# Taps of a convolution read from PSUM, roots of three norms on GpSimd, a residual in another buffer

## The chip, the cores and the metric

The kernel runs on one core of one Trainium2 chip. The metric is the time of one execution on the device, in microseconds, the median of several runs. In the texts PE is TensorE, ACT is ScalarE, DVE is VectorE, POOL is GpSimd, and SP is the queue that issues the DMAs.

## The reference

4096 tokens (two sequences of 2048, 256 wide) pass four blocks, all in float32.

1. A selective state space block (Mamba). `xn = layer_norm(x)`, `xz = xn @ W_in`, split into `x_br` and `z` of 512 channels each. A causal depthwise convolution of 4 taps along time, `xb = silu(conv(x_br) + conv_b)`. From `xb` come `Bm`, `Cm` (16 states) and `delta = softplus(xb @ W_delta + b_delta)`. Then the recurrence `h = exp(delta * A) * h + delta * Bm * xb`, `y = sum(h * Cm)` over the 16 states, and `out = ((y + xb * Dp) * silu(z)) @ W_out + residual`.
2. A layer norm around a mixture of 4 experts with 2 chosen per token (router of one hidden layer, experts 256 to 1024 to 256, exact gelu).
3. An attention block of 16 heads of width 16, whose keys get an additional product term (`cross`).
4. A feed-forward block with its layer norms.

The convolution needs, for the first three tokens of a chunk, the last three of the chunk before, or zeros at the start of a sequence.

## The kernel before, in words

The program has two halves. The first, `mamba_moe_qkv`, does blocks 1 and 2 and the projections q, k, v of block 3, in 8 chunks of 512 tokens. The second half does attention and the feed-forward block; the change does not touch it.

The first half is a software pipeline whose order is written out by hand for each engine. In iteration `i` (from -1 to 9) the recurrence of chunk `i` runs in 16 slots `n`, one per state. In between stand the input side (norm, projection, convolution, delta) of chunk `f = i + 1`, the experts of chunk `m = i - 1` and q, k, v of chunk `q = i - 2`. Each engine goes through its instructions in order and waits on semaphores.

A slot of DVE is: `b_times` of half 0 (line 919, 128x1024, PSUM), two scans (line 930), whatever is placed in the middle of the slot, `b_times` and two scans of half 1, and `keep_state` (line 937); then what is placed at the end of the slot. POOL multiplies `h` by the row of C for that state (`times_c`, line 1132) and adds it to `y_sum` (`add_y`, line 1143); `h` has two buffers, so the scans of slot n need the sum of slot n-2. ACT makes the decays of slot n+1 (line 669) at the start of its slot n. PE makes the broadcast of a row of B (line 382) for slot n+2 at the end of slot n.

The parts that matter here, before the change:

- Layer norm (`layer_norm`, lines 53 to 87), wholly on DVE: four `bn_stats` (69), four `bn_aggr` (72), thirteen operations on 128x4 values for the inverse root (lines 75 to 82: a seed from the bits and three Newton steps), and four applies (84). norm0 is the input norm, of chunk `i + 2` at the end of slot 12; norm1 is of chunk `m` at the end of slot 2; norm2 of chunk `q` at the end of slot 1.
- The residual: `load_residual` (line 266) is issued by SP in slot 2, behind `load_c(i, 4)`, which waits for POOL's product of slot 2. It goes into `x1_tok`, the buffer in which norm1, the experts' sums and norm2 work. Line 948 adds it to the output projection (lines 435 to 446, `project_out`, PE in slot 1).
- Banks 4 and 5 of PSUM serve in turn `project_out`, the turning of x1 (`turn_x1`, 448), z (`project_z`, 405), the turning of xn (`turn_xn`, 385), the x projection (`project_x`, 394), the keys' addition (`add_keys`, 569, line 580), and the experts' `down` (502, line 518). The z projection and the silu gates stand in slot 3 on PE and ACT, `turn_xn` in slot 4, behind `turn_x1`; the x projection of blocks 0 and 1 in slot 4 behind `cross`, of blocks 2 and 3 in slot 5, ahead of `router` (456).
- The convolution: ACT copies each projected block from PSUM twice (`copy_x`, 692): as it is into `x_br`, three columns in (699), and scaled by the last tap's weight into `xb` (700). `halo` (860, DVE) puts the last three columns of the chunk before, or zeros, ahead of it. `conv` (868) adds the other three taps: twelve `scalar_tensor_tensor` per chunk (line 879), `xb += w * x_br[shifted]`, six at the end of slot 7 and six at the end of slot 9. ACT's silus (703) follow in slot 11. `x_br` is also the buffer `pre` of the delta projection (721).
- The experts' `up` (492) goes through banks 6 and 7 with ACT's gelu (740); `down` from slot 7 on; its results are read by DVE at line 1015 in the middle of slots 8 to 13 and 0, 1 of the next iteration.

## Time and profile before

| | us |
|---|---|
| median of 3 runs (lowest, highest) | 4282.59 (4281.64, 4284.22) |
| the profiled execution: its own time | 4292.46 |
| its span in the profile | 4290.5 |
| busy: PE, DVE, ACT, POOL | 3558.7, 3161.5, 2212.4, 1513.9 |
| DVE, line 879, the taps, x96 | 147.6 |
| DVE, lines 75 to 82 in the first half, the 4-element steps of the norms, x312 | 144.9 |
| DVE idle ahead of line 948, waiting for the residual's DMA, x8 | 86.1 |
| DVE idle ahead of line 1015, waiting for PE's `down` | 258.0 |

The profile's rows are read so: line, engine, operation, output and inputs by their names in the program, shapes, count, busy time and mean duration, then the idle time of the engine just before the group and who ended it. In a timeline, neighbouring instructions of one line are merged into one row (x4 is four of them), with the idle time ahead in brackets. Idle time of an engine that isn't the bound costs nothing.

### The profile page before, as it was taken

The numbers are of one execution on the slowest core, as the hardware profiler recorded it, in microseconds if no ns is written. First come the engines' busy times: TensorE is split into PE (matmuls) and PEld (weight loads), VectorE is DVE, ScalarE is ACT, GpSimd is POOL, SyncE is SP. The second block draws the span as 40 slices with busy tenths as digits, with TensorE's granted clock in tenths as the row PEclk, the third lists the DMA queues.
The fourth block names the chain that finished last, engine by engine and source line by source line (L and its number), as shares of the span: only waits on it lengthen the run. The fifth ranks groups of instructions, "written<-read, shape, count | busy, mean of one in ns | idle before, by whom it ended". The sixth has DMA issues, their size and how long they took to land. (4 is left out here: it accounts for less than half of the span.)

```text
span 4290.5 us, 50229 instructions
## 1 busy us (share of the span) xinstructions
PE 3558.7 (83%) x14625; PEld 1618.9 (38%) x14625; DVE 3161.5 (74%) x3753; ACT 2212.4 (52%) x3556; POOL 1513.9 (35%) x1140
## 2 busy tenths in 40 slices
PE   4228778697786987868896799999999999999898
PEld 1015435344353443534553132323222232323565
DVE  5988777887778877777512887878778787878443
ACT  4335544455444544445321277777777777777221
POOL 2977666676666766667611000000000000000110
PEclk7669889898898997988998699999999999999999
DMA  2011212212122121121210200000000000000001
GB/s 93 28 32 44 65 39 77 62 55 72 42 73 65 45 76 45 62 74 50 91 55 25 89 22 17 16 17 24 17 17 16 17 24 17 16 17 19 30 29 34
DMA packets 110769, 183.17 MB, mean 43 GB/s; under 512 B 14495, under 2 KB 84599, under 8 KB 101817
## 3 DMA queue, kind: packets, MB, share of 16 engines
q1 hardware_dynamic: 110521, 180.09, 13.4%
q8 instruction: 128, 2.10, 0.2%
q14 instruction: 120, 0.98, 0.1%
HBM read 153.95 MB, written 26.09 MB: 42 GB/s over the span
## 5 line engine op out<-in xcount | busy, mean ns | idle before, releaser
L1588 DVE TENSOR_REDUCE tile_max<-ps 128x1 f32<-128x1024 f32 x1076 | 1268.3, 1220 | 291.3 <-PE ps L1379 288.6
L1533 ACT ACTIVATE probs<-ps 128x512 f32<-128x512 f32 x2056 | 1119.0, 600 | 493.9 <-PE ps L1393 469.3
L1132 POOL TENSOR_TENSOR h<-h,c_sb 128x512 f32<-128x512 f32 x512 | 696.7, 1391 | 672.3 <-DVE state L937 672.3
L1393 PE MATMUL ps<-qs,ks 101*128 101x512 bf16 x2056 | 714.1, 385 | 1.3
L1379 PE MATMUL ps<-ks,qs 99*128 99x512 bf16 x2152 | 669.6, 393 | 48.9 <-DMA ks<-scratch_kb 41.1
L1143 POOL TENSOR_TENSOR y_sum<-y_sum,h 128x512 f32<-128x512 f32 x512 | 665.2, 1330 | 10.3 <-POOL h L1132 0.5
L930 DVE TENSOR_TENSOR_SCAN h<-decay,state,ps 128x512 f32<-128x512 f32 x512 | 627.5, 1267 | 44.5 <-POOL y_sum L1143 15.1
L498 PE MATMUL ps<-x1T,e_w 128*128 128x512 f32 x1024 | 527.6, 669 | 96.2 <-ACT hid L740 95.8
L1403 PE MATMUL ps<-probs,vh 128*32 128x512 f32 x4096 | 553.5, 613 | 24.6 <-issue 24.6
L1705 POOL COPY vh<-v_all 128x256 f32 (+1 forms) x32 | 12.7, 402 | 1437.2 <-PE ps L1403 1371.7
L518 PE MATMUL ps<-e_w,hid 128*128 128x256 f32 x2048 | 454.1, 380 | 11.3 <-ACT hid L740 7.5
L740 ACT ACTIVATE hid<-ps,cols 128x512 f32<-128x512 f32 x288 | 194.1, 688 | 485.8 <-PE ps L498 462.0
L1393 PEld LDWEIGHTS ps<-qs,ks 101*128 101x128 bf16 x2056 | 199.1, 97 | 646.1 <-ACT probs L1533 436.5
L669 ACT ACTIVATE decay<-delta,neg_a 128x512 f32<-128x512 f32 x512 | 335.9, 715 | 159.4 <-DVE h L930 149.4
L518 PEld LDWEIGHTS ps<-e_w,hid 128*128 128x128 f32 x2048 | 386.7, 190 | 83.1 <-issue 29.4
L498 PEld LDWEIGHTS ps<-x1T,e_w 128*128 128x128 f32 x1024 | 215.4, 215 | 389.4 <-issue 260.2
L919 DVE TENSOR_TENSOR ps<-du,ps 128x1024 f32<-128x1024 f32 x256 | 313.1, 1223 | 8.0 <-PE ps L382 3.3
L1379 PEld LDWEIGHTS ps<-ks,qs 99*128 99x128 bf16 x2152 | 209.0, 99 | 274.8 <-issue 51.4
L1015 DVE SCALAR_TENSOR_TENSOR x_tok<-ps,cw,x_tok 128x256 f32<-128x256 f32 x128 | 55.2, 473 | 258.0 <-PE ps L518 258.0
L382 PE MATMUL ps<-bc,sel 96*128 96x512 bf16 x128 | 54.4, 427 | 205.3 <-DVE ps L919 205.2
L1403 PEld LDWEIGHTS ps<-probs,vh 128*32 128x32 f32 x4096 | 81.2, 108 | 221.5 <-ACT probs L1533 180.1
L879 DVE SCALAR_TENSOR_TENSOR xb<-x_br,cols,xb 128x512 f32<-128x512 f32 x96 | 147.6, 1602 | 10.7 <-ACT xb L700 10.3
(172 smaller groups left out, 3115.1 us busy)
## 6 DMA issues: line engine op xcount, KB each, us to landing
e_w<-in_e_w SPq DMA_DIRECT2D x64, 1024.0 KB, 7.0
c_sb<-scratch_c SPq DMA_DIRECT2D x128, 256.0 KB, 3.5
qs<-scratch_q SPq DMA_DIRECT2D x210, 64.0 KB
ks<-scratch_k SPq DMA_DIRECT2D x210, 64.0 KB
scratch_q<-parts SPq DMA_DIRECT2D x16, 384.0 KB, 4.0
scratch_k<-parts SPq DMA_DIRECT2D x16, 384.0 KB, 7.4
xr<-scratch_x SPq DMA_DIRECT2D x10, 512.0 KB, 4.0
xn_tok<-in_x SPq DMA_DIRECT2D x8, 512.0 KB, 4.8
```

The lines of the kernel that those rows point to most:

```text
L498: last = mm(bank(key), e_w1[:, e % 2, k, i * P:(i + 1) * P], x1T[:, k, :], start=k == 0, stop=k == KD - 1)
L518: last = mm(ps[:, DOWN_BANK[at], i * D:(i + 1) * D], hid[:, k, (2 * pair + i) * P:(2 * pair + i + 1) * P], e_w2[:, e % 2, k, :], start=k = ...
L669: fn(decay[:, n % 2, m, :], delta[:, m, :], ACT.Exp, scale=neg_a[:, n * DB + m:n * DB + m + 1]).then_inc(s["decay_ready"], 1)
L919: v.tensor_tensor(ps[:, 0:2, :], du[:, 2 * half:2 * half + 2], ps[:, 2 + n % 2:3 + n % 2, :].to_broadcast([P, 2, CH]), ALU.mult)\
L930: v.tensor_tensor_scan(h[:, n % 2, m, :], decay[:, n % 2, m, :], ps[:, m % 2, :], state[:, n, m:m + 1], ALU.mult, ALU.add)\
L1132: last = nc.gpsimd.tensor_tensor(h[:, n % 2, m, :], h[:, n % 2, m, :], c_sb[:, n % C_RING, :], ALU.mult)
L1143: last = nc.gpsimd.tensor_tensor(y[:, m, :], y[:, m, :], h[:, n % 2, m, :], ALU.add)
L1379: last = mm(ps[:, slot(side) + i, :], qs[0:K_MAX, j, t * P:(t + 1) * P], ks[0:K_MAX, j, k * CH:(k + 1) * CH], start=True, stop=True)
L1393: mm(ps[:, S_BANK[i], :], ks[0:K_ALL, j, step * P:(step + 1) * P], qs[0:K_ALL, j, qc * CH:(qc + 1) * CH], start=True, stop=True).then_inc( ...
L1403: last = mm(ps[qc * VW:(qc + 1) * VW, AV_BANK, :], vh[:, j, step, :], probs[:, step % 2, qc, :], start=step == 0, stop=step == KT - 1)
L1533: fn(probs[:, step % 2, qc, :], ps[:, S_BANK[i], :], ACT.Exp)\
L1588: v.tensor_reduce(tile_max[:, t, half:half + 1], ps[:, slot(side):slot(side) + PAIR, :].rearrange("p a n -> p (a n)"), AX.X, ALU.max).then ...
```

## The change

1. **Norms.** `layer_norm` of the first half is split in two: `norm_stats` (bn_stats, bn_aggr) and `norm_apply`. The inverse root becomes two operations on POOL, an addition of eps and a power with exponent -0.5 (`scale`), placed between POOL's product and its sum of a slot. The statistics move to the middle of DVE's slot, the applies stay at its end.
2. **Convolution.** `x_br` is gone; the taps read the projection in banks 4 and 5, and write `xb` from column `back` on. ACT copies only the last three columns of each block (`halo`). What the first three tokens need from the chunk before is worked out on POOL (`mix_edge`, six small operations in slot 1) and added to `xb` by one more (`add_edge`, slot 8). conv pair 0 moves to the end of slot 4, pair 1 to the middle of slot 6. PE's x projection of blocks 2 and 3 waits for conv pair 0 and stands behind the router; the keys' addition stands behind the up of slot 6.
3. **Order.** The z projection and its gates move from slot 3 to slot 2, ahead of q, k and `turn_x1`; `turn_xn` from slot 4 to slot 3; the x projection of blocks 0 and 1 stands ahead of `cross`.
4. **Residual.** It is loaded in slot 1, ahead of `load_c(i, 3)`, into columns of `hid`.
5. `pre` gets a buffer of its own.

```diff
+def norm_stats(nc, dve, steps, c, src, tmp, passed):
+    stats, mv = tmp[0], tmp[1]
+    n = src.shape[1]
+    for i in range(n):
+        last = nc.vector.bn_stats(stats[:, i, :], src[:, i, :])
+    last.then_inc(steps, 1)
+    wait_alone(dve, passed, steps, c * NORM_STEPS + 1)
+    for i in range(n):
+        last = nc.vector.bn_aggr(mv[:, i, :], stats[:, i, :])
+    last.then_inc(steps, 1)
+
+def norm_apply(nc, steps, src, dst, tmp):
+    mv, r = tmp[1], tmp[5]
+    for i in range(src.shape[1]):
+        last = nc.vector.tensor_scalar(dst[:, i, :], src[:, i, :], mv[:, i, 0:1], r[:, i:i + 1],
+                                       ALU.subtract, ALU.mult)
+    last.then_inc(steps, 1)
...
             def load_residual(c):
-                at_least(sp, s["ln2_steps"], c * LN_STEPS)
-                sp.dma_start(x1_tok[:], ...)
+                at_least(sp, s["down_mm"], c * 2 * NE)
+                sp.dma_start(residual, ...)
...
                 for n in range(NS):
+                    if n == 1 and inside(m):
+                        load_residual(m)
                     if inside(i) and n + 2 < NS:
                         load_c(i, n + 2)
                     if n == 1 and inside(m):
                         load_w2(m, 1)
-                    if n == 2 and inside(m):
-                        load_residual(m)
...
             def project_x(c, blocks):
                     else:
-                        pe.wait_ge(s["tap_ready"], c * DB + e - 1)
+                        pe.wait_ge(s["conv_steps"], c * CONV_STEPS + CONV_STEPS // 2)
...
             def turn_xn(c):
+                at_least(pe, s["x1T_ready"], c - 1)
...
             def project_z(c):
-                at_least(pe, s["x1T_ready"], c)
+                at_least(pe, s["r_ready"], c)
...
             def turn_x1(c):
+                pe.wait_ge(s["gate_ready"], upto(c + 2) * DB)
...
             def add_keys(c, i):
-                    pe.wait_ge(s["tap_ready"], (i + 2) * DB)
+                    pe.wait_ge(s["conv_steps"], (i + 2) * CONV_STEPS)
...
@@ tensor, iteration(i)
-                    if n == 2 and inside(q):
-                        turn_x2(q)
-                        project_v(q)
+                    if n == 2:
+                        if inside(q):
+                            turn_x2(q)
+                            project_v(q)
+                        if inside(i):
+                            project_z(i)
                     if n == 3:
                         if inside(q):
                             project_qk(q)
                         if inside(m):
                             turn_x1(m)
-                        if inside(i):
-                            project_z(i)
+                        if inside(f):
+                            turn_xn(f)
                     if n == 4:
                         if inside(f):
-                            turn_xn(f)
+                            project_x(f, (0, 1))
                         if inside(q):
                             cross(q)
-                        if inside(f):
-                            project_x(f, (0, 1))
                     if n == 5:
+                        if inside(m):
+                            router(m)
                         if inside(f):
                             project_x(f, (2, 3))
-                        if inside(m):
-                            router(m)
-                    if n == 6 and inside(q):
-                        add_keys(q, i)
...
+                    if n == 6 and inside(q):
+                        add_keys(q, i)
...
             def copy_x(c, blocks):
-                    fn(x_br[:, e, TAPS - 1:], ps[:, 4 + e % 2, :], ACT.Copy).then_inc(s["xbr_copied"], 1)
+                    fn(halo[:, e, :], ps[:, 4 + e % 2, CH - TAPS + 1:], ACT.Copy)
...
             def conv(c, pair):
                 for tap in range(TAPS - 1):
+                    back = TAPS - 1 - tap
...
-                        v.scalar_tensor_tensor(xb[:, e, :], x_br[:, e, tap:tap + CH], col("conv_w", tap * DB + e),
-                                               xb[:, e, :], ALU.mult, ALU.add).then_inc(s["conv_steps"], 1)
+                        v.scalar_tensor_tensor(xb[:, e, back:], ps[:, 4 + j, 0:CH - back], col("conv_w", tap * DB + e),
+                                               xb[:, e, back:], ALU.mult, ALU.add).then_inc(s["conv_steps"], 1)
...
@@ vector, iteration(i), middle of the slot
+                    if n == 1 and inside(q):
+                        norm2_stats(q)
+                    if n == 2 and inside(m):
+                        norm1_stats(m)
+                    if n == 12 and inside(i + 2):
+                        norm0_stats(i + 2)
...
+                    if n == 6 and inside(f):
+                        conv(f, 1)
@@ vector, iteration(i), end of the slot
-                        norm2(q)
+                        norm2_apply(q)
...
-                        norm1(m)
-                    if n == 3 and inside(f) and inside(i):
-                        halo(f)
+                        norm1_apply(m)
...
-                    if n in (7, 9) and inside(f):
-                        conv(f, (n - 7) // 2)
+                    if n == 4 and inside(f):
+                        conv(f, 0)
...
-                        norm0(i + 2)
+                        norm0_apply(i + 2)
...
@@ gpsimd
+            def mix_edge(c):
+                for tap in range(TAPS - 1):
+                    nc.gpsimd.tensor_tensor(edge[:, tap, :, 0:TAPS - 1 - tap], halo[:, :, tap:],
+                                            cols[:, k:k + DB].unsqueeze(2).to_broadcast([P, DB, TAPS - 1 - tap]),
+                                            ALU.mult).then_inc(steps, 1)
...
+            def add_edge(c):
+                pool.wait_ge(s["conv_steps"], (c + 1) * CONV_STEPS)
+                pool.wait_ge(s["edge_steps"], (c + 1) * EDGE_STEPS)
+                nc.gpsimd.tensor_tensor(xb[:, :, 0:TAPS - 1], xb[:, :, 0:TAPS - 1], edge[:, 0], ALU.add)\
+                    .then_inc(s["edge_added"], 1)
...
+            def scale(name, c):
+                pool.wait_ge(s[name + "_steps"], c * NORM_STEPS + 2)
+                nc.gpsimd.tensor_tensor(ln_tmp[2], ln_tmp[1][:, :, 1], powers[:, 0], ALU.add)\
+                    .then_inc(s[name + "_scaled"], 1)
+                pool.wait_ge(s[name + "_scaled"], c * 2 + 1)
+                nc.gpsimd.tensor_tensor(ln_tmp[5], ln_tmp[2], powers[:, 1], ALU.pow)\
+                    .then_inc(s[name + "_scaled"], 1)
...
                     if inside(i):
                         times_c(i, n)
+                    if n == 0 and inside(q):
+                        scale("ln2", q)
+                    if n == 1 and inside(m):
+                        scale("ln1", m)
+                    if n == 11 and inside(i + 2):
+                        scale("ln0", i + 2)
+                    if inside(i):
                         add_y(i, n)
+                    if n == 1 and inside(f):
+                        mix_edge(f)
+                    if n == 8 and inside(f):
+                        add_edge(f)
```

## Rows read from the trace of the kernel before

**Rows 1.** Busy time by stage; columns stretch, length, engines, granted clock, DMA share, GB/s

```profile
0.00:271.00 271.00, 80.84 (x163) 32.36 (x163) 210.90 (x242) 107.50 (x150) 167.87 (x133) 0.68 0.15 52
271.00:521.00 250.00, 186.79 (x580) 109.78 (x580) 194.27 (x218) 119.09 (x161) 170.20 (x128) 0.85 0.18 55
...
1067.00:1340.00 273.00, 216.26 (x642) 121.22 (x642) 220.82 (x256) 128.50 (x175) 184.71 (x136) 0.86 0.19 60
...
1880.00:2118.00 238.00, 188.78 (x575) 108.92 (x575) 165.45 (x203) 98.14 (x133) 174.47 (x136) 0.87 0.21 69
...
1067.00:1097.00 30.00, 14.68 (x45) 10.66 (x46) 28.85 (x41) 7.26 (x11) 21.68 (x16) 0.61 0.18 59
...
1272.00:1315.00 43.00, 39.15 (x108) 19.59 (x107) 41.28 (x51) 18.51 (x26) 23.14 (x17) 1.00 0.24 80
```

**Rows 2.** Timeline of DVE in one middle iteration

```profile
1067.23 2.29 DVE L943 TENSOR_TENSOR gate<-y_sum,gate 128x2048 f32<-128x2048 f32 x1
...
1080.12 0.57 DVE L75 TENSOR_SCALAR ln_ve<-ln_mv 128x4 f32<-128x4 f32 x1
...
1090.18 1.38 DVE L84 TENSOR_SCALAR x_tok<-x_tok,ln_mv,ln_r 128x256 f32<-128x256 f32 x4
...
1111.06 1.22 DVE L948 SCALAR_TENSOR_TENSOR x_tok<-x_tok,ps 128x1024 f32<-128x1024 f32 x1 [11.63 <-DMA x_tok<-in_x]
...
1272.25 0.88 DVE L1015 SCALAR_TENSOR_TENSOR x_tok<-ps,cw,x_tok 128x256 f32<-128x256 f32 x2 [19.61 <-PE ps L518]
...
1278.87 0.76 DVE L75 TENSOR_SCALAR ln_ve<-ln_mv 128x4 f32<-128x4 f32 x1
...
1289.99 1.38 DVE L84 TENSOR_SCALAR xn_tok<-xn_tok,ln_mv,ln_r 128x256 f32<-128x256 f32 x4
...
1340.29 2.29 DVE L943 TENSOR_TENSOR gate<-y_sum,gate 128x2048 f32<-128x2048 f32 x1
```

**Rows 3.** Timeline of PE in the same iteration

```profile
1073.97 9.77 PE L444 MATMUL ps<-w_out,gate 128*128 128x256 f32 x32 [8.84 <-DVE x_tok L1015]
...
1091.62 1.97 PE L535 MATMUL ps<-ident,x_tok 128*128 128x128 f32 x8 [7.66 <-DVE x_tok L84]
...
1121.49 9.87 PE L413 MATMUL ps<-xnT,w_in 128*128 128x512 f32 x16 [1.21 <-ACT x1T L736]
...
1157.70 3.83 PE L468 MATMUL ps<-r_w,hid 128*128 128x4 f32 x32 [0.78 <-ACT hid L740]
...
1190.05 7.14 PE L518 MATMUL ps<-e_w,hid 128*128 128x256 f32 x32
...
1204.15 7.03 PE L498 MATMUL ps<-x1T,e_w 128*128 128x512 f32 x16
...
1311.74 3.60 PE L431 MATMUL ps<-xb,w_delta 128*128 128x512 f32 x8
```

**Rows 4.** Groups of instructions on DVE, window 1067 to 1340; count, busy us, mean ns

```profile
L930 DVE TENSOR_TENSOR_SCAN h<-decay,state,ps 128x512 f32<-128x512 f32 x64 | 78.5, 1268 | 2.8 <-ACT decay L669 1.4 <-POOL y_sum L1143 0.3
L919 DVE TENSOR_TENSOR ps<-du,ps 128x1024 f32<-128x1024 f32 x32 | 39.1, 1223 | 1.4 <-PE ps L382 0.6 <-DVE x_tok L84 0.4 <-DVE xn_tok L84 0.2
L879 DVE SCALAR_TENSOR_TENSOR xb<-x_br,cols,xb 128x512 f32<-128x512 f32 x12 | 20.4, 1763 | 0.1
L1015 DVE SCALAR_TENSOR_TENSOR x_tok<-ps,cw,x_tok 128x256 f32<-128x256 f32 x16 | 6.9, 474 | 21.8 <-PE ps L518 21.8
```

**Rows 5.** Timeline of POOL, at the start and in slot 5 of a middle iteration

```profile
80.71 4.95 POOL L1132 TENSOR_TENSOR h<-h,c_sb 128x512 f32<-128x512 f32 x4 [80.25 <-DVE state L937]
...
1160.27 2.12 POOL L1160 TENSOR_TENSOR q_f<-q_f,parts 128x1024 f32<-128x1024 f32 x1
```

**Rows 6.** Timeline of DVE at the start, with POOL idle

```profile
30.73 7.38 DVE L879 SCALAR_TENSOR_TENSOR xb<-x_br,cols,xb 128x512 f32<-128x512 f32 x11 [1.28 <-ACT xb L700]
```

**Rows 7.** Timeline of ACT, a table load and four decays

```profile
1132.01 1.28 ACT L669 ACT_TABLE_LOAD   x1
1133.30 2.57 ACT L669 ACTIVATE decay<-delta,neg_a 128x512 f32<-128x512 f32 x4
```

129 lines of the change are left out of this document (79 added, 50 removed).

## The prediction

> **What bounds the kernel now.** I read three views in this order: busy time by stage, the DVE timeline of one middle iteration, then the PE timeline of the same stretch. The profiled execution took 4292.46 us, 9.9 above the runs' median of 4282.59; the sum is made against its own time and the difference is taken off at the end. [rows 1] cuts the first half at the `gate` products of line 943, one per iteration. In the iteration from 1067 to 1340 PE is busy 216 of 273 us, DVE 221, POOL 185: no engine is full, so two chains alternate. [rows 2] shows them on DVE. The last state product of slot 0 ends at 1067.23 (G below), the next at 1340.29: a period of 273.1. DVE loses 11.63 us to the residual's DMA, which is issued behind the C row that waits for POOL, and 19.61 us in slot 12 to the second expert's `down`. Before the second wait DVE is early and PE is the bound; after G, PE waits for DVE [rows 3]: `project_out` starts 6.7 us after G, x2's transposes (L535) wait for norm2, x1's for norm1 (they come just ahead of L413). So early in an iteration DVE's norms and the DMA set PE's chain, later PE's chain sets everything.
>
> **The change, part by part.** *Norms.* DVE's thirteen 4-element steps take 10.1 us in norm2 (1080.12 to 1090.18) and 11.1 in norm0 (1278.87 to 1289.99) [rows 2]; in norm1, while POOL is idle, the same steps need 2.6 us by the start of its applies. They go away. In their place POOL does an add and a power between its product and its sum, while DVE runs half a slot: two L919 halves and four scans are 2 x 1.22 + 4 x 1.27 = 7.5 us, half of it 3.75 [rows 4]. No row shows a small POOL operation. 512 elements take about 4.94 / 4 = 1.24 us, 1024 take 2.12 [rows 5]: on that line a 4- or 12-element one costs 0.35. The bounds are nothing and the 2.12 of 1024 elements; I take 0.4, as these are nearest to the short end. Two of them (0.8) hide behind the 3.75, and are no cost to DVE while they stay under it.
>
> *Residual.* It goes ahead of C row 3 in SP's queue, into `hid`, free since the last `down`. It is issued at about G+8, lands before G+17, and is wanted at G+18: the 11.63 go. One DMA moves, no queue gets a longer wait: its semaphore (all earlier `down`s) is set before G.
>
> *Convolution.* 12 steps of 1.763 us (20.4 per iteration, L879) [rows 4]. With POOL idle, at the start, eleven of them take 7.38 us, 0.67 each [rows 6]: the rest of the price is the meeting with POOL. A step of the same operation with one operand in PSUM takes 0.474 for 256 elements (L1015) and 1.22 for 1024 (L948) with POOL at work: 0.73 for 512 on that line. Bounds 0.67 and 1.763; I take 0.73, since L1015 has exactly the new form. A pair costs 4.4 instead of 10.6, 12.4 us less DVE per iteration. The Trainium skill, "VectorE: DVE Perf Modes", section "Rules for kernel authors", says the opposite: with many operations on a matmul's result, copy it from PSUM to SBUF first. That would make the old order the cheaper one; L1015 and L948 in this trace disagree with it. ACT saves four full copies and makes four 3-column ones. The edge adds six small POOL operations in slot 1 (2.5 us at 0.4) and one in slot 8.
>
> *What is given for it.* Banks 4 and 5 are held by the taps: `project_x(2, 3)` waits for conv pair 0 on DVE, the keys' product and all PE work queued behind it for pair 1. In the first iteration nothing covers this: projection, tap, conv, projection, tap, conv in series is about 6.5 us longer, less 1.5 for the first norm: **+5**.
>
> **A middle iteration laid out anew**, in us after G, with durations of [rows 2, 3, 4, 7]. DVE: gate 2.2, first half of slot 1 5.9, `down` 6.7, norm2's statistics 8.7, slot 1 done 12.6, apply 14.2, half 17.9, residual sum and statistics 21.2, slot 2 and apply 26.7 (before, the residual sum alone began at 43.8). Slot 3 ends at 34.4. POOL: product 0 ends 7, stats come 8.7, sum 0 14.7, product 1 19.7, root 22.2, sum 1 27.2, edge 29.5, product 2 34.5, sum 2 39.5; scan 4 needs that sum, so DVE waits about 4 us and slot 4 ends at 46. POOL takes over as bound there, briefly.
> PE: `project_out` to 16.5 (9.77), x2 turned and v projected to 25.8 at the durations shown, z to 35.7 (9.87). ACT: silu and a table load, 4 decays (1.28 + 2.57) [rows 7] to 40.2, then v's copy; q and k to 48, x1 and xn turned and copied to 54.5, x blocks 0 and 1 to 58.2, cross to 66.9. ACT's gelu load cannot start before decays 6 at 69.8; from it to the logits takes 10.35 as before: 80.2 against 94.3 (1157.70 + 3.83 - 1067.23). x blocks 2 and 3 end at 83.8, ups and keys follow, the first `down` starts at 109.2 against 122.8 (L518 at 1190.05): **-13.6**. DVE: pair 0 waits for ACT's taps until 57.8 and ends at 62.6, slot 5 with cross at 75.2, logits at 82, pair 1 at 88, the router's weights at 98.7, slot 7 with the keys at 108. Neither waits long for the other.
> This keeps PE's cold durations. [rows 1] has the granted clock at 0.61 from 1067 to 1097, between its two levels 1.2 and 2.4 GHz, and PE has gaps of 7 us before both turnings. The new order leaves only short gaps from G+7 to G+58. At full clock 16 matmul rows of the same form as z take 7.03 (L498) instead of 9.87 [rows 3]; So z saves 2.8, x2's and x1's turning (1.97 each at the low level) 1 each, and by the same ratio v 2 and the first up 3, together 9.7 us: first `down` at 99.5, **-23.3**.
> From there PE runs the same 82 us to slot 12 (L1015's row): DVE's saved conv there only lengthens its wait. Behind slot 12 norm0 leaves DVE, 11.1, but PE's delta chain (L431 at 1311.74, then softplus, then `delta`) was waited for at the same moment, so only PE's own wait for DVE of 2.4 goes. Per middle iteration -16.0 cold, -25.7 warm. I take **-21**, a little to the warm side of the middle, because most gaps on PE close.
>
> **Sum.** Start +5. Iteration 0: POOL is the bound (its chain starts at 80.71 [rows 5], 32 groups of 4.94 = 158); with 3 of added small operations and some 5 lost to meetings with DVE's two-operand steps it ends at 247, the gate product at 253 instead of 271: -18. Iteration 1 (250 us [rows 1], DVE waits longest for the residual, no third chunk's work on PE): logits after about 56 instead of 81, first `down` 23 earlier, and the 2.4: -25. Iterations 2 to 6: 5 x 21 = -105. Iteration 7 (238 us), without a convolution: -15, its end bound by POOL's sums. Iterations 8 and 9: norms without POOL's load, -4. The attention half has no edit. Together -162: 4292.5 - 162 = 4130 in that execution, **4121** against the median. Cold everywhere it is -124 (4159), warm everywhere about -200 (4083).
>
> **Rivals.** (a) *Taps from PSUM are no cheaper*, the rule above taken at its word, at 1.763 each: a pair is 6.2 longer, pair 1 ends at 89 instead of 83, `weigh` 8 later; the first `down` moves by about 5 in eight iterations: 4121 + 40 = 4161. Against it: L1015. 8%. (b) *POOL becomes the bound.* At 2.12 per small operation, ten of them in slots 0 to 2 push scan 4 by 17, conv pair 0 by 5 to 12, and iteration 0 takes 20 more: 4121 + 7 x 8 + 20 = 4197. Against it: POOL is idle 88 us of 273. 12%. (c) *The early gain is lost on PE*: the logits come no sooner, as z now stands ahead of q, k and x1; then only the 2.4 and iteration 0 stay, 35 us, 4248. For it: DVE already waits for PE in slot 12, and PE is the bound for a third of the iteration. 8%. (d) *Slower*: the banks' chain. PE's queue stops at `project_x(2, 3)` and at the keys until DVE has done a conv that itself stands behind a scan, the logits and POOL's sum. It decides once the two holds together exceed 21 us, that is if pair 0 ends after G+86 instead of 55 to 63, or pair 1 after 104 instead of 81 to 88. Two holds of a loaded slot, 13 us each, give +5 per iteration: 4121 + 8 x 26 = 4329. 5%. (e) Gains eaten exactly, within 0.2% (about what a measurement of this kernel can tell from no change): 3%.
>
> **How the numbers follow.** The forecast, cold to warm, holds 64%: 4121. The range goes from beyond the warm end, 4075, to rival (b), 4205; (c), (d), (e) stay out with 16%. Faster 92%, same 3%, slower 5%.
>
> **What would show it.** DVE: L943 to L943 about 252 us apart; conv steps near 0.73; the residual wait gone; the 19.6 wait in slot 12 kept or longer, now above 25. POOL: small operations near 0.4, scan 4 waiting for a sum of y. PE: fewer gaps before logits, granted clock above 0.61 in the first 30 us after G. A long idle time of PE ahead of the x projection or the keys' product, released by the conv, would speak for (d); DVE idle behind POOL in many slots for (b).

## The result, and the profile after it

Four runs of the changed kernel gave a median of 4110.44 us (4107.91 to 4113.52), those of the kernel before on the same chip 4283.27. The ratio is 0.9597, with a 95% interval of 0.9581 to 0.9614: 4.0% less, 173 us. The prediction had 4121, with a range of 4075 to 4205. The profiled execution has a span of 4111.7 us, against 4290.5 before. That of before was 9 us above its median and that of the changed kernel 3, so the two spans differ by 178.8, 6 more than the medians.

First the engines' shares of the whole span, as the page of the changed kernel has them:

```profile
PE 3500.6 (85%) x14625; PEld 1599.7 (39%) x14625; DVE 2964.8 (72%) x3436; ACT 2195.3 (53%) x3556; POOL 1515.1 (37%) x1244
```

Then the busy time by stage of the changed kernel, cut at the gate products (now line 976) as in [rows 1]; the columns are stretch, length, PE, PEld, DVE, ACT, POOL, granted clock, DMA share and GB/s.

```profile
258.00:488.00 230.00, 188.91 (x580) 111.99 (x580) 172.67 (x192) 117.25 (x160) 168.38 (x139) 0.89 0.18 60
982.00:1228.00 246.00, 201.56 (x642) 115.47 (x642) 191.77 (x217) 126.67 (x176) 183.78 (x149) 0.93 0.21 67
982.00:1012.00 30.00, 21.22 (x67) 13.20 (x68) 29.22 (x40) 11.16 (x18) 23.77 (x20) 0.82 0.21 70
1228.00:1482.00 254.00, 209.45 (x642) 119.00 (x642) 193.29 (x215) 126.35 (x175) 183.61 (x149) 0.90 0.21 65
```

A middle iteration of before had 216.3 us of PE at a granted clock of 0.86 and 220.8 of DVE [rows 1]. Now the same 642 matmuls take 201.6 at 0.93, and DVE 191.8. The first 30 us after the gate product (G) went from 0.61 to 0.82. The two iterations shown have the same work and differ by 8 us: PE's clock is 0.93 in one and 0.90 in the other. That is the noise between iterations, against which the parts below have to be read.

Between gate products the periods are 230.2, 243.8, 249.5, 246.2, 254.4, 248.1 and 216.5 us; before they were 250.1, 273.5, 272.7, 273.1, 270.1, 269.3 and 238.2.

DVE's timeline in the iteration that begins at 981.72, to lay beside [rows 2]; columns are start, us, engine, line and operation, with the wait before it in brackets:

```profile
981.72 2.29 DVE L976 TENSOR_TENSOR gate<-y_sum,gate 128x2048 f32<-128x2048 f32 x1
...
994.43 4.99 DVE L110 TENSOR_SCALAR x_tok<-x_tok,ln_mv,ln_r 128x256 f32<-128x256 f32 x4 [0.18 <-issue]
...
1002.96 1.20 DVE L982 SCALAR_TENSOR_TENSOR x_tok<-hid,ps 128x1024 f32<-128x1024 f32 x1
...
1024.53 2.45 DVE L963 TENSOR_TENSOR_SCAN h<-decay,state,ps 128x512 f32<-128x512 f32 x2 [1.51 <-POOL y_sum L1192]
...
1036.47 3.37 DVE L912 SCALAR_TENSOR_TENSOR xb<-ps,cols,xb 128x509 f32<-128x509 f32 x5 [0.97 <-ACT xb L739]
...
1163.32 0.88 DVE L1052 SCALAR_TENSOR_TENSOR x_tok<-ps,cw,x_tok 128x256 f32<-128x256 f32 x2 [16.16 <-PE ps L555]
...
1188.45 1.19 DVE L920 CAST bc<-bc_f 96x512 bf16<-96x512 f32 x1 [7.97 <-PE ps L417]
...
1210.81 4.36 DVE L937 SCALAR_TENSOR_TENSOR delta<-pre,soft 128x1024 f32<-128x1024 f32 x2 [1.37 <-ACT soft L771]
...
1227.88 2.29 DVE L976 TENSOR_TENSOR gate<-y_sum,gate 128x2048 f32<-128x2048 f32 x1
```

The wait for the residual's DMA, 11.63 us before, is gone: the sum at 1002.96 starts with no wait. The last of norm2's applies ends at G+17.7 (24.3 before), the residual's sum starts at G+21.2 (43.8 before). From slot 12 on DVE waits 16.16, 7.97 and 1.37 us, for PE, PE and ACT: in the second half these two set the pace.

Groups of instructions on DVE in the window 982 to 1228, with the columns of [rows 4]:

```profile
L110 DVE TENSOR_SCALAR x_tok<-x_tok,ln_mv,ln_r 128x256 f32<-128x256 f32 x8 | 8.3, 1101 | 0.2 <-issue 0.2
L110 DVE TENSOR_SCALAR xn_tok<-xn_tok,ln_mv,ln_r 128x256 f32<-128x256 f32 x4 | 4.3, 1124 | 0.0
...
L912 DVE SCALAR_TENSOR_TENSOR xb<-ps,cols,xb 128x509 f32<-128x509 f32 x4 | 3.0, 747 | 8.2 <-ACT xb L739 8.2
...
L912 DVE SCALAR_TENSOR_TENSOR xb<-ps,cols,xb 128x510 f32<-128x510 f32 x4 | 2.8, 740 | 0.0
```

A convolution step is 0.74 us, where it was 1.76. The norms' applies went the other way: norm2's four take 4.99 us together, where they took 1.38 before [rows 2], and a single one has a mean of 1.10, where all of them had 0.41 before. Without the thirteen small steps ahead of them they now stand beside POOL's sum and product.

POOL's timeline at norm2 and norm1 of the same iteration:

```profile
990.46 0.20 POOL L1249 TENSOR_TENSOR ln_ve<-ln_mv,powers 128x4 f32<-128x4 f32 x1 [1.64 <-DVE ln_mv L101]
990.74 1.02 POOL L1252 TENSOR_TENSOR ln_r<-ln_ve,powers 128x4 f32<-128x4 f32 x1
991.73 5.00 POOL L1192 TENSOR_TENSOR y_sum<-y_sum,h 128x512 f32<-128x512 f32 x4
...
1012.44 0.90 POOL L1204 TENSOR_TENSOR edge<-halo,cols 128x12 f32<-128x12 f32 x3
```

An add of 4 elements takes 0.20 us, the power 1.02, an edge product of 12 elements 0.30 (three in 0.90).

PE's timeline of the same stretch, to lay beside [rows 3]:

```profile
988.45 9.21 PE L479 MATMUL ps<-w_out,gate 128*128 128x256 f32 x32 [8.84 <-DVE x_tok L1052]
...
999.47 1.09 PE L572 MATMUL ps<-ident,x_tok 128*128 128x128 f32 x8 [1.59 <-DVE x_tok L110]
1001.30 3.70 PE L563 MATMUL ps<-x1T,wqkv 128*128 128x512 f32 x8 [0.74 <-ACT x1T L802]
1004.84 7.03 PE L449 MATMUL ps<-xnT,w_in 128*128 128x512 f32 x16
...
1053.49 3.73 PE L504 MATMUL ps<-r_w,hid 128*128 128x4 f32 x32 [0.78 <-ACT hid L779]
...
1084.44 7.14 PE L555 MATMUL ps<-e_w,hid 128*128 128x256 f32 x32
...
1200.11 3.60 PE L466 MATMUL ps<-xb,w_delta 128*128 128x512 f32 x8
```

x2 is turned at G+17.8 (24.4 before), after a gap of 1.6 us instead of 7.7, and in 1.09 us instead of 1.97; z takes 7.03 instead of 9.87. The logits end at G+75.5 (94.3 before), the first `down` starts at G+102.7 (122.8).

**Where the time went, in one table.** Marks in us after G, each taken from PE's and DVE's timelines of one middle iteration of the kernel named (its G in the first column). "Slot 12" is the start of DVE's read of the `down` that it waits for there; the last column is from there to the next G. Several experiments stand in it already.

| kernel, G | logits end | first `down` | slot 12 | next G | slot 12 to next G |
|---|---|---|---|---|---|
| before, 1067 | 94.3 | 122.8 | 205.0 | 273.1 | 68.1 |
| after, 982 | 75.5 | 102.7 | 181.6 | 246.2 | 64.6 |
| after, 1228 | 78.8 | 107.7 | 189.9 | 254.4 | 64.5 |
| roots on DVE, 1031 | 90.3 | 119.2 | 201.4 | 268.5 | 67.1 |
| norm0's root on DVE, 1005 | 75.5 | 105.4 | 187.4 | 254.6 | 67.2 |
| norm2's root on DVE, 1003 | 79.5 | 109.5 | 191.6 | 256.1 | 64.5 |
| residual behind C row, 1009 | 83.4 | 115.0 | 197.1 | 261.7 | 64.6 |
| taps from SBUF, 1008 | 79.9 | 107.7 | 188.1 | 252.6 | 64.5 |
| before + residual, 1040 | 86.2 | 114.7 | 196.8 | 264.9 | 68.1 |
| norm2 in slot 0, 983 | 76.1 | 105.1 | 187.2 | 254.5 | 67.3 |

Against before, the iteration of 246.2 wins 20.1 by the first `down`, 3.3 between that and slot 12, and 3.5 behind slot 12; the one of 254.4 wins 15.1, 0 and 3.6. The last part is the same in both; the first two are larger in the iteration in which PE's clock was higher. On the mean of iterations 2 to 6 the first `down` comes 18.3 sooner (122.0 to 103.7), the stretch from it to slot 12 is 1.7 shorter and that behind slot 12 3.3: the 23.3 us between periods of 271.7 and 248.4.

### The profile page after: what moved, and what is told of

Same layout as the page of the kernel before. It is cut to its first block and busy times, and to the rows that moved or that the text cites. A ratio compares the mean times of both kernels' runs of the same rounds, so it can differ in the third digit from the quotient of the medians.

```text
span 4111.7 us, 49896 instructions
## 1 busy us (share of the span) xinstructions
PE 3500.6 (85%) x14625; PEld 1599.7 (39%) x14625; DVE 2964.8 (72%) x3436; ACT 2195.3 (53%) x3556; POOL 1515.1 (37%) x1244
## 5 line engine op out<-in xcount | busy, mean ns | idle before, releaser
L1181 POOL TENSOR_TENSOR h<-h,c_sb 128x512 f32<-128x512 f32 x512 | 678.7, 1356 | 421.9 <-DVE state L970 421.8
L1192 POOL TENSOR_TENSOR y_sum<-y_sum,h 128x512 f32<-128x512 f32 x512 | 641.3, 1284 | 8.5
L534 PE MATMUL ps<-x1T,e_w 128*128 128x512 f32 x1024 | 491.6, 629 | 103.0 <-ACT hid L779 102.6
L534 PEld LDWEIGHTS ps<-x1T,e_w 128*128 128x128 f32 x1024 | 202.4, 202 | 365.0 <-issue 225.7
L1052 DVE SCALAR_TENSOR_TENSOR x_tok<-ps,cw,x_tok 128x256 f32<-128x256 f32 x128 | 55.2, 473 | 270.4 <-PE ps L555 270.4
L417 PE MATMUL ps<-bc,sel 96*128 96x512 bf16 x128 | 53.8, 421 | 169.6 <-DVE ps L952 169.6
L479 PE MATMUL ps<-w_out,gate 128*128 128x256 f32 x256 | 76.7, 473 | 67.0 <-DVE x_tok L1052 62.7
```

The costliest lines, as they stand in the source:

```text
L534: last = mm(bank(key), e_w1[:, e % 2, k, i * P:(i + 1) * P], x1T[:, k, :], start=k == 0, stop=k == KD - 1)
L1181: last = nc.gpsimd.tensor_tensor(h[:, n % 2, m, :], h[:, n % 2, m, :], c_sb[:, n % C_RING, :], ALU.mult)
L1192: last = nc.gpsimd.tensor_tensor(y[:, m, :], y[:, m, :], h[:, n % 2, m, :], ALU.add)
```

## The experiments

All ratios are to the kernel before, run on the same chip as the experiment. "Against after" is the difference of two ratios times 4283 us, so that chips cancel out. With the intervals of both ratios put together it is good to about 12 us either way, 15 for norm2 in slot 0 and 19 for the gap filled in the changed kernel.

| run | median us | ratio, 95% interval | against after |
|---|---|---|---|
| changed kernel | 4110.4 | 0.9597 (0.9581 to 0.9614) | |
| all roots on DVE | 4224.5 | 0.9876 (0.9852 to 0.9899) | +119 |
| norm0's root on DVE | 4148.5 | 0.9691 (0.9671 to 0.9711) | +40 |
| norm2's root on DVE | 4151.8 | 0.9699 (0.9681 to 0.9717) | +44 |
| residual behind the C row | 4164.9 | 0.9733 (0.9710 to 0.9756) | +58 |
| taps from SBUF | 4155.4 | 0.9719 (0.9697 to 0.9741) | +52 |
| z behind q and k | 4136.1 | 0.9672 (0.9650 to 0.9694) | +32 |
| norm2 in slot 0 | 4122.5 | 0.9642 (0.9611 to 0.9674) | +19 |
| after, gap filled | 4125.7 | 0.9633 (0.9593 to 0.9673) | +15 |
| delta chain first | 4086.2 | 0.9559 (0.9542 to 0.9576) | -16 |
| before + residual | 4221.6 | 0.9872 (0.9850 to 0.9893) | |
| before, gaps filled | 4310.2 | 1.0078 (1.0058 to 1.0099) | |
| before, gaps filled in full iterations only | 4277.6 | 1.0005 (0.9991 to 1.0019) | |

**1. The roots.** The theory was that PE's chain behind the gate product sets the period, and that DVE's small steps stand ahead of it. All three norms' roots go back to DVE, ahead of the applies:

```diff
 def norm2_apply(c):
-    dve.wait_ge(s["ln2_scaled"], 2 * c + 2)
+    dve.wait_ge(s["ln2_steps"], c * NORM_STEPS + 2)
+    norm_root(nc, dve, s["ln2_scaled"], c, ln_tmp)
     at_least(dve, s["x2_stored"], 16 * c)
```

and the same for norm0 and norm1; `norm_root` is the old thirteen steps, and POOL's `scale` returns at once.

> The changed kernel (4110 us) with all three norms' roots back on DVE (13 small steps each, just ahead of the applies). Theory (PE's chain after the gate product sets the period): norm2's 10 us lie ahead of x2's turning and open a gap on PE that lowers its clock; norm1's 10 us are half covered by q and k on PE; norm0's 10 us lie behind slot 12, where DVE has about 9 us of waiting. +12 to +18 per iteration, 4195 to 4240. Rival (DVE's busy time sets the period): 30 us per iteration come back on DVE, so about 4310 or more.

4224.51 us: within the theory's span and far below the rival's, so DVE's busy time by itself doesn't set the period. 119 of the 173 us are tied to this part. Logits come at G+90.3, and slot 12 to the next G takes 67.1. The marks show two places where it is paid, ahead of PE's early chain (norm2, norm1) and behind slot 12 (norm0). Two more runs take them apart, each with one norm's root on DVE.

> The changed kernel with only norm0's root back on DVE, at the end of slot 12. Theory: covered by DVE's waits behind slot 12 (8.0 for a broadcast, 1.4 for the softplus), 0 to +3 per iteration, 4110 to 4135. Rival (DVE's busy time): +10 per iteration, about 4190.

4148.51 us, outside both expectations: +40, some 5 per iteration. DVE's timeline of this kernel behind slot 12:

```profile
1193.11 0.88 DVE L1076 SCALAR_TENSOR_TENSOR x_tok<-ps,cw,x_tok 128x256 f32<-128x256 f32 x2 [17.60 <-PE ps L578]
...
1220.06 1.50 DVE L944 CAST bc<-bc_f 96x512 bf16<-96x512 f32 x1 [0.19 <-PE ps L440]
```

The wait of 7.97 us for the broadcast is down to 0.19, so it covers most of the root's steps (12.5 us from first to last), and the 1.37 before `delta` is gone; what sticks out costs 2.6 us between slot 12 and the next G (67.2 against 64.6). I had taken the cover as complete. Not all of the 40 is paid there: of the 35 us that the profiled executions show, 8 come before the first G, at 266.57 where it was 258.23, and in iteration 0 there is no `down` to wait for.

> The changed kernel with only norm2's root back on DVE, at the end of slot 1. Theory: all of it ahead of x2's turning on PE, which waits 1.6 us already, so +9 to +14 per iteration in seven iterations, 4175 to 4205. Rival (DVE's busy time): about +10, the same as for norm0's root alone; the two theories part on the difference between this run and that one.

4151.75 us, +44. The median is below the theory's span (4175 to 4205), and the two single roots cost the same within the noise (+40 and +44), which is what the rival had for their difference; its size, about +10 per iteration, is not. In this place the thirteen steps take about 6.5 us, and the applies behind them fall back from 4.99 us to about 1.4, since POOL is past its product by then. x2 is turned only 3.0 us later than in the changed kernel. But look at PE's timeline of this kernel:

```profile
1024.20 1.97 PE L595 MATMUL ps<-ident,x_tok 128*128 128x128 f32 x8 [4.00 <-DVE x_tok L133]
1026.86 6.53 PE L586 MATMUL ps<-x1T,wqkv 128*128 128x512 f32 x8 [0.69 <-ACT x1T L825]
1033.23 7.03 PE L472 MATMUL ps<-xnT,w_in 128*128 128x512 f32 x16
```

After a gap of 4.0 us instead of 1.6, the turning takes 1.97 instead of 1.09 and v 6.53 instead of 3.70, so z starts 6.7 later from a delay of 3.0. A short gap here costs its own length and PE's clock behind it (granted 0.55 during v, where the changed kernel has 1.00). It is so in every iteration with this work, 2 to 7: in the changed kernel PE waits 0.5 to 1.8 us ahead of x2's turning and v takes 3.7 in all six; with norm2's root on DVE it waits 3.5 to 4.3, and v takes 5.2 to 6.6. The two single runs together give +84, all three roots +119; norm1's was not run alone.

**2. The residual.** Only its place in SP's queue changes. It goes behind C row 3, in slot 1; in the kernel before it stood behind C row 4, in slot 2, so this is less than the old order, and the new buffer stays:

```diff
-    if n == 1 and inside(m):
-        load_residual(m)
     if inside(i) and n + 2 < NS:
         ...
+    if n == 1 and inside(m):
+        load_residual(m)
```

> The changed kernel with the residual's DMA behind C row 3 in SP's queue, so behind POOL's product of slot 1. Theory: it lands about 5 us after DVE wants it, and z on PE waits for the sum: +4 to +6 per iteration, 4142 to 4160. Rival (the transfer is hidden anyway, DVE's idle time costs nothing): 4105 to 4116.

4164.92 us, just above the theory's span and far above "hidden". DVE's sum in this kernel:

```profile
1034.58 1.22 DVE L982 SCALAR_TENSOR_TENSOR x_tok<-hid,ps 128x1024 f32<-128x1024 f32 x1 [4.18 <-DMA hid<-in_x]
```

The wait is 4.18 us and not 11.63, with an earlier C row ahead of it. In seven iterations it is 4.1 to 8.8 us, 37 together, and the kernel pays 58 (51 by the profiled executions): more than the waits themselves. The opposite test is the residual alone on the kernel before, into `hid[:, 2:4]` and a slot earlier:

```diff
+residual = hid[:, 2:4, :].rearrange("p a (s n) -> p (a s) n", n=D)
-    at_least(sp, s["ln2_steps"], c * LN_STEPS)
-    sp.dma_start(x1_tok[:], a["x"][bass.ds(c * CH, CH), :].rearrange("(s p) n -> p s n", p=P))\
+    at_least(sp, s["down_mm"], c * 2 * NE)
+    sp.dma_start(residual, a["x"][bass.ds(c * CH, CH), :].rearrange("(s p) n -> p s n", p=P))\
...
+    if n == 1 and inside(m):
+        load_residual(m)
...
```

> The kernel before (4283 us) with the residual alone as in the change: another buffer, issued in slot 1 ahead of the C row. Theory: norm1 comes 11.6 us sooner on DVE, but PE's gap ahead of x1's turning is 6.8 us and it is PE's chain that counts: -6 to -9 per iteration, 4215 to 4240. Rival (every us of DVE counts): -11.6 in eight iterations, 4190.

4221.59 us, 0.9872: the theory's span. It takes the 11.63 away and gives 8.2 per iteration (logits 94.3 to 86.2). The residual is worth 55 us in the old kernel; in the new one it would cost 58 to put it only one C row back.

**3. The taps.** ACT also copies the projection to SBUF (`x_sb`, the delta projection's buffer `pre`), and the taps read that copy:

```diff
+fn(x_sb[:, e, :], ps[:, 4 + e % 2, :], ACT.Copy)
-v.scalar_tensor_tensor(xb[:, e, back:], ps[:, 4 + j, 0:CH - back], col("conv_w", tap * DB + e),
+v.scalar_tensor_tensor(xb[:, e, back:], x_sb[:, e, 0:CH - back], col("conv_w", tap * DB + e),
```

> The changed kernel with the taps read from a copy in SBUF: ACT copies each block in full as well, conv reads that copy; places and waits unchanged. Theory: a step takes 1.2 to 1.76 us instead of 0.73, a pair 3 to 6 us longer; pair 0 partly covered, pair 1 delays the keys' product on PE: +3 to +6 per iteration, 4130 to 4160. Rival 1 (DVE's busy time): +12 per iteration, 4205. Rival 2 (many operations on a matmul's result are cheaper from SBUF): 4110 or below.

4155.38 us, as expected, +52. DVE's timeline of this kernel, the five steps that follow each other in pair 0 and in pair 1:

```profile
1061.79 7.64 DVE L914 SCALAR_TENSOR_TENSOR xb<-pre,cols,xb 128x509 f32<-128x509 f32 x5 [0.71 <-ACT xb L741]
...
1094.58 3.39 DVE L914 SCALAR_TENSOR_TENSOR xb<-pre,cols,xb 128x509 f32<-128x509 f32 x5 [1.45 <-ACT xb L741]
```

And POOL's timeline of it at these moments:

```profile
1060.45 6.76 POOL L1183 TENSOR_TENSOR h<-h,c_sb 128x512 f32<-128x512 f32 x4
...
1089.66 2.12 POOL L1240 TENSOR_TENSOR q_f<-q_f,parts 128x1024 f32<-128x1024 f32 x1
```

Beside POOL's product five steps take 7.64 us, 1.53 each, and the product itself is lengthened from some 5.0 to 6.76; with POOL done at 1091.8 five steps take 3.39. From PSUM five take 3.37, and a single one 0.72 to 0.75 in all 96 cases, POOL busy or not. So PSUM is no faster by itself; the gain is in the meeting, in both directions. The copies that ACT has more of are not what costs the time here: the second step of pair 0 starts at G+53.8 (54.8 in the changed kernel). Behind the longer pair DVE's product for the keys is late, ACT's table load for the router's gelus waits 5.33 us for it instead of 1.25, and the logits end at G+79.9 instead of 75.5. The prediction weighed a rule from the Trainium skill ("VectorE: DVE Perf Modes", "Rules for kernel authors"): either accept the slower read from PSUM, or copy a matmul's result to SBUF first when many operations follow. Its second half would have had this version the faster one. In this kernel it is 52 us slower: the measurement decides against it here.

**4. z's place.** In the change, z is projected between v and q/k. This run puts it behind them, and ACT's `gates(i)` behind `copy_qk(q)`:

```diff
     if n == 3:
         project_qk(q)
+        if inside(i):
+            project_z(i)
```

> The changed kernel with the z projection and its gates behind q and k again (but ahead of x1's turning). Theory: PE's work up to the x projection is the same in another order, the 3.9 us wait ahead of q goes and another of the same kind comes: 4095 to 4125. Rival (z's earlier place is what gives the early gain): +8 or more per iteration, 4175.

4136.13 us, +32, of which the profiled execution, 4125.4 in span, shows 14. It falls between the two expectations: z's earlier place is worth 2 to 4 us per iteration and is not what carries the change.

**5. Is it PE's clock?** The prediction gave the closing of gaps a share of its own (-16 cold, -25.7 warm). If that is a cause by itself, idle matmuls put into the old gaps should bring part of the gain. They stand ahead of x2's turning (8) and of x1's (7). Their results go to a bank that is written anew and are used by nothing:

```diff
+def fill(c, keys, n):
+    for key in keys:
+        wait_free(pe, c, key)
+    for j in range(n):
+        mm(bank(keys[0]), w_in[:, 0, 0:P], xnT[:, 0, :], start=True, stop=True)
...
+    fill(q, [("x2T", 0)], 8)
...
+    fill(q, [("cross", 0)], 7)
```

> The kernel before with idle matmuls (results unused) in two gaps of PE: 8 ahead of x2's turning, 7 ahead of x1's, where PE waits 7.7 and 6.8 us for DVE. Theory: the granted clock stays at its high level, so x2's turning, v, z and x1's turning take up to 7 us less: -4 to -8 per iteration in seven iterations, 4225 to 4255. Rival (the clock is no part of the gain, only the order and the waits are): 4278 to 4300.

4310.16 us: slower, outside both expectations. In the profiled execution iterations 2 to 6 are 1 to 6 us shorter, but what follows the last G, where PE has no such gap, is 27 us longer. The first of these readings is weak: this execution was 9 us below its kernel's median and that of before 9 above. So the fill was cut to the iterations that have the gap:

> As e8, the kernel before with idle matmuls in PE's two gaps, but not in the last two iterations, where PE has no such gaps and the matmuls only add their own time. Theory (the granted clock is a part of the gain): the middle iterations 3 to 6 us shorter, nothing lost at the end, 4250 to 4270 against about 4280. Rival (only order and waits count): 4275 to 4290.

Ten runs: 4277.59 us, 1.0005 (0.9991 to 1.0019). No gain, as the rival had it. Busy time by stage just after G, first of the filled kernel, then of the kernel before over the same 25 and 30 us:

```profile
1064.00:1089.00 25.00, 17.21 (x53) 11.29 (x54) 23.99 (x37) 6.02 (x9) 21.72 (x16) 0.76 0.20 68
1089.00:1119.00 30.00, 21.05 (x63) 10.29 (x62) 17.02 (x36) 10.00 (x16) 9.88 (x8) 0.91 0.18 44
```

```profile
1067.00:1092.00 25.00, 10.37 (x35) 8.31 (x36) 23.95 (x37) 6.07 (x9) 21.68 (x16) 0.64 0.22 71
1092.00:1122.00 30.00, 18.91 (x50) 9.62 (x49) 17.32 (x36) 10.42 (x16) 9.89 (x8) 0.78 0.15 44
```

The clock did rise, from 0.64 to 0.76 and from 0.78 to 0.91, in part on the idle matmuls themselves. The time did not fall; the logits still come at G+94.6. PE's timeline of the filled kernel (its G is at 1064.19) shows why:

```profile
1115.60 1.97 PE L459 MATMUL ps<-ident,x_tok 128*128 128x128 f32 x8 [4.62 <-DVE x_tok L84]
1118.78 9.66 PE L420 MATMUL ps<-xnT,w_in 128*128 128x512 f32 x16 [1.21 <-ACT x1T L747]
```

x1's turning waits for DVE's norm1 and starts at G+51.4, where it was 51.1: DVE and the DMA, not PE, set it. But the second gap is still 4.62 us long, and z behind it takes 9.66 (9.87 before, 7.03 in the change) at the same granted clock (0.73 and 0.72). So this run shows that a faster PE ahead of norm1 brings nothing; what a z at the full clock would bring in the old order, it does not test. The same was tried on the changed kernel, with 8 idle matmuls ahead of `project_out`:

> The changed kernel with 8 idle matmuls on PE ahead of the output projection, where it waits 8.8 us for DVE. Theory: the output projection falls from 9.2 to about 7.2 us and PE's chain behind it starts at the high clock: -2 to -6 per iteration, 4065 to 4098. Rival (the wait for DVE's norm2 and norm1 takes it up): 4105 to 4116.

4125.72 us, 0.9633 (0.9593 to 0.9673), above both expectations by the median, but the interval holds the changed kernel's 0.9597: no gain, and no loss that is clear of the noise. PE's timeline of this kernel (its G is at 996.36):

```profile
1003.10 7.17 PE L486 MATMUL ps<-w_out,gate 128*128 128x256 f32 x32
...
1014.11 1.09 PE L579 MATMUL ps<-ident,x_tok 128*128 128x128 f32 x8 [3.62 <-DVE x_tok L110]
1015.94 6.72 PE L570 MATMUL ps<-x1T,wqkv 128*128 128x512 f32 x8 [0.74 <-ACT x1T L811]
...
1068.48 5.78 PE L511 MATMUL ps<-r_w,hid 128*128 128x4 f32 x32 [0.78 <-ACT hid L788]
```

`project_out` takes 7.17 us instead of 9.21, as was wanted. But x2's turning starts at G+17.8, just as in the changed kernel, since norm2's applies on DVE end then: the wait ahead of it grew from 1.59 to 3.62 and took up what was won. Behind it v takes 6.72 instead of 3.70 (granted clock 0.54), as it does with norm2's root on DVE; in all of iterations 2 to 7 the wait is 3.5 to 3.6 and v takes 5.2 to 6.7. The idle matmuls did not close PE's gap, they moved it ahead of x2. What makes the logits' group slow (5.78 instead of 3.73), with no wait above 0.8 us just ahead of it, stays open.

**6. Is it a loop?** If each period is one loop (DVE's `delta`, slots 0 and 1, norm2, norm1, PE's early chain to the first `down`, PE to slot 12, its delta projections, ACT's softplus, DVE's `delta`), then moving DVE work from one side of G to the other must bring nothing, and taking a wait out of the loop must bring time. For the first, both `down` reads, norm2's statistics and its applies go into slot 0, ahead of G, and POOL's root ahead of its product:

```diff
-    if n < 2 and inside(q):
-        down(q, NE - 1, n)
-    if n == 1 and inside(q):
+    if n == 0 and inside(q):
+        down(q, NE - 1, 0)
+        down(q, NE - 1, 1)
         norm2_stats(q)
...
```

> The changed kernel with DVE's reading of the last down product and norm2's statistics in the middle of slot 0 instead of slot 1, norm2's applies at the end of slot 0, and its root on POOL ahead of the product of slot 0. Theory: the output projection on PE starts 4 us sooner after the gate product, x2's turning 6 us sooner, z about 3 (it then waits for the residual sum): -2 to -5 per iteration, 4070 to 4097. Rival (DVE's work and POOL's sums set the period): no less work on either, 4105 to 4118.

4122.48 us, 0.9642 (0.9611 to 0.9674): none of the gain that the theory had (4070 to 4097), and a few us beyond the rival (4105 to 4118); at best a tie. PE's timeline of this kernel (its G is at 983.29):

```profile
985.73 9.80 PE L479 MATMUL ps<-w_out,gate 128*128 128x256 f32 x32 [4.53 <-DVE gate L976]
995.85 1.04 PE L572 MATMUL ps<-ident,x_tok 128*128 128x128 f32 x8
999.83 3.70 PE L563 MATMUL ps<-x1T,wqkv 128*128 128x512 f32 x8 [2.94 <-ACT x1T L802]
```

`project_out` starts 2.4 us after G instead of 6.7, x2 is turned at G+12.6 instead of 17.8. That is the early start I wanted. But slot 12 to the next G takes 67.3 instead of 64.6: the work now stands ahead of G, in the same loop. The mean of iterations 2 to 6 says it without the noise of one: slot 12 comes 2.0 us sooner than in the changed kernel, and from there to the next G it is 2.7 longer.

For the second, the wait of 7.97 us in slot 13 is looked at. DVE wants a broadcast there, which in PE's queue stands behind an up-projection, and `delta`'s last projection stands behind another. Both are moved ahead (the first two conditions below are PE's, the last ACT's), and softplus on ACT ahead of the second up's evictions:

```diff
+    if n == 14:
+        project_delta(f, 3)
+    if n == 13 and inside(i):
+        broadcast(i, 15)
...
+    if n == 14:
+        copy_delta(f, 3)
+        softplus(f)
...
```

> The changed kernel with the delta chain ahead of the fourth expert's up: on PE the last delta projection stands ahead of up(3, 1) and the broadcast of slot 15 ahead of up(3, 0); on ACT the last delta copy and the softplus stand ahead of up(3, 1)'s gelus. Theory as the runs so far leave it (the period is a loop through DVE's delta, slot 0, the gate product, norm2, norm1, PE's early chain to the first down, PE to slot 12, PE and ACT to the softplus): the softplus ends about 8 us sooner, DVE's wait of 8.0 for the broadcast in slot 13 goes, the gate product comes 4 to 7 us sooner, and the downs still end before DVE reads them: 4060 to 4090. Rival (PE's total work sets the period, no part of it went): the fourth down is late by the gelus' delay and is waited for after the gate product, 4105 to 4125.

Five runs: 4086.16 us (4080.89 to 4090.54), 0.9559 (0.9542 to 0.9576). This is within the theory's span (4060 to 4090), at its upper end, and the interval of the ratio lies wholly below that of the changed kernel, so this version beats both. DVE's timeline of it:

```profile
1180.65 0.42 DVE L925 CAST bc<-bc_f 96x512 bf16<-96x512 f32 x1
...
1215.34 2.45 DVE L968 TENSOR_TENSOR_SCAN h<-decay,state,ps 128x512 f32<-128x512 f32 x2 [2.74 <-ACT decay L712]
1218.63 0.88 DVE L1057 SCALAR_TENSOR_TENSOR x_tok<-ps,cw,x_tok 128x256 f32<-128x256 f32 x2 [0.84 <-PE ps L555]
...
1223.41 2.29 DVE L981 TENSOR_TENSOR gate<-y_sum,gate 128x2048 f32<-128x2048 f32 x1
```

The waits of 7.97 and 1.37 are gone. Two new ones, 2.74 for ACT's decays and 0.84 for PE, take part of it back. The softplus ends 9.6 us sooner, counted from slot 12, but middle iterations average 246.4 against 248.4, and iteration 1 is 7.6 shorter. On the mean of iterations 2 to 6 the stretch behind slot 12 is 4.4 shorter, while slot 12 itself comes 2.4 later after G. Most of that is v again: in four of the five iterations PE waits 2.1 to 2.2 us ahead of x2's turning, and v takes 5.4 instead of 3.7. So both tests speak for the loop in their direction, and neither gives its size.

## Why the prediction was nearly right

**The picture of the bound was right.** Early in an iteration DVE's norms and the DMA set PE's chain, later PE sets everything: undoing the roots or the residual costs time, and PE made faster ahead of norm1 alone gives none. What the prediction lacked is that the two halves close to a loop through PE's delta chain, so that DVE's work behind slot 12 counts too. It said of norm0 that only PE's own wait of 2.4 goes. The measured part behind slot 12 is 3.5 in the iteration of 246.2 (3.3 in the mean), and undoing norm0's root alone costs 2.6 there and +40 in all.

**The sum, term by term** (spans; predicted, then measured as differences of the G marks):

| term | predicted | measured |
|---|---|---|
| start and iteration 0 | +5 - 18 = -13 | -12.8 |
| iteration 1 | -25 | -19.9 |
| iterations 2 to 6 | 5 x -21 = -105 | -116.6 (-23.3 each) |
| iteration 7 | -15 | -21.8 |
| iterations 8, 9 and the rest | -4 | -7.7 |
| sum | -162 | -178.8 |

By medians it is 161 predicted and 173 measured. The start's +5 is there by itself: slot 0's first product on DVE is at 77.60 us, 72.67 before. The largest miss is the middle iteration: "I take -21", between cold and warm, came out at 23.3. Its parts, as means of iterations 2 to 6: the first `down` moved by 18.3, where cold was 13.6 and warm 23.3; "from there PE runs the same 82 us to slot 12" was 80.5; behind slot 12 it was 3.3 and not 2.4. That 18.3 lies between the two marks does not show by itself that PE was warm for half of it, as other steps of the layout were off too, in both directions (below). The sum's ends of -124 and -200 can't be had from its terms: with -16 and -25.7 in the five middle iterations it would be -137 and -186. In iteration 7 the end is bound by POOL's sums, as said (DVE waits 11.6 us for the last one, 10.5 before), but those sums start sooner too: the first `down` starts at G+92.3 instead of 112.9 (-20.6), slot 12 comes 21.8 sooner, and from there to the end it is 46.8 in both. In iteration 1 the logits end at G+55.2 instead of 81.2, as laid out (56), but the first `down` follows only at 85.6 instead of 103.8: -18.2, not the 23 that the step "first `down` 23 earlier" carried on from the logits. From logits to `down` PE now needs 30.4 us instead of 22.5: 5.42 of it is the x projection of blocks 2 and 3, which the change puts behind the router, and 2.9 are longer waits for ACT. The layout of the middle iteration had that projection there; the term of iteration 1 left it out.

**The steps, one by one.**
- *Small operations on POOL at 0.4 each.* The adds were below (0.20), the edge's too (0.30), the power was 1.02. The pair of 1.2 us stayed under the half slot of 3.75: in the whole first half DVE waits 7.1 us for roots, in five places. The conclusion held though one size was off by 2.5 times.
- *Norms' applies.* The layout had the last of norm2's end at G+14.2, it is 17.7. The applies, four in 1.38 us before, cost 4.99 there, as they now stand beside POOL's sum and product. With norm0's and norm1's it is 8.5 us of DVE per iteration that no step of mine had (norm2's 3.6 lie straight ahead of x2's turning), and the copies of the state behind the scans grew by another 3.4 (5.3 to 8.7). The residual's sum came at G+21.2 where it was to be wanted at 18.
- *Taps at 0.73.* 0.742. L1015 was the right row to take. The lower bound of 0.67 was the distance from one step to the next (7.38 / 11), not the duration of one, which is 0.74 from SBUF too with POOL idle; steps from PSUM follow each other at 0.67 as well (3.37 / 5).
- *Residual.* Issued at G+7.9, landed 4.6 us later, no wait. Right.
- *Logits at 80.2 cold.* 75.5 and 78.8. Slot 4's scan waits 1.5 us for POOL, not 4, and ACT's table load for the gelus stands at G+65.3, not 69.8; from it to the logits it is 10.2, as laid out (10.35).
- *DVE's wait in slot 12 "kept or longer, now above 25".* Wrong: 16.16, where it was 19.61. I counted all of DVE's saved convolution into that one wait, but 8.2 us are spent waiting for ACT's taps, 6.41 for the `down` in slot 10 (1.03 before) and 7.97 in slot 13 (0.19 before), which I had not seen coming. The last is the one whose removal made the last experiment the fastest.

**The rivals.** (a) falls with 0.742 us a step. (b) falls: POOL's largest small operation is 1.02, and DVE waits 1.5 us for y's sums in the iteration shown. (c) falls: the logits came 15 to 19 us sooner in the iterations of the table, with z ahead of q and k; moving z back costs time. (d), the banks' chain: conv pair 0 ends at G+58.1 and pair 1 at G+85.0, against thresholds of 86 and 104; the waits around them are 2.95, 0.97, 3.01 and 1.23 us, DVE's for ACT, and no long wait of PE's. (e) is excluded by the interval.

**The clock.** That PE runs at a higher granted clock with fewer gaps is what the rows show (0.86 to 0.93, 14.7 us less busy time for the same matmuls). The prediction made it a cause. How much of the time is due to it is not shown. The fill runs say that it brings nothing where DVE and the DMA set the pace, ahead of norm1 in the old kernel and ahead of x2's turning in the new one; in the old kernel they did not raise it for z, to which the prediction gave 2.8 us (z did fall from 9.87 to 7.03). Why one iteration has 0.93 and its twin 0.90 is not settled by any run here.

## What to carry to other kernels

When no engine is full, look for the loop that closes from one iteration to the next and ask of each edit whether it shortens the loop, moves work along it, or stands beside it. Here a wait of 11.6 us taken out gave 8.2 per iteration, one of 8 at the delta chain gave 2, and work moved along the loop gave nothing. A run that moves work along the suspected loop tells what one that removes work can't. Where two engines meet on the same memory, price an instruction from a row in which the same neighbour is at work: here the tap read from PSUM was steady at 0.74 us while from SBUF it was anything from 0.74 to 1.84, and the norm's apply went from 0.41 us to as much as 1.43 merely by standing elsewhere. And when a gap is filled with idle work, see whether the gap is closed or has only moved, and whether the work behind it got faster, before the result is read as a verdict on the clock.

## What was unexpected in the hardware

- POOL's power on 4 elements per partition takes 1.02 us, five times an add of the same size (0.20).
- DVE's instructions of a few elements lengthen beside a busy POOL by up to seven times: with norm2's root on DVE, steps of 4 elements take 1.12 to 1.19 us each from 1016.3 to 1021.0, where POOL's product ends, and 0.16 each from then on. In the changed kernel the state copy of 4 elements (L970) has a mean of 0.55 us in the iteration shown, with single ones from 0.16 to 1.91.
- The same group of 8 matmuls of the x projection takes 3.70 us at one place of an iteration and 6.63 at another (the changed kernel with its gap filled, 1048.08 and 1074.12; granted clock 1.00 and 0.55), and from the one to the other PE never waits longer than 0.8 us.
